# A decoder layer on one core: layer norm a slot ahead, PV of self-attention a slot back, maximum, output copy and PV in another order

## The chip, the cores and the metric

The kernel runs on one core of a Trainium2 chip. The time is device time in microseconds (us) of one execution, median over runs. The core has five engines with queues of their own: TensorE (PE, matmuls; PEld is its weight load), VectorE (DVE), ScalarE (ACT), GpSimd (POOL) and SyncE (SP, which starts the DMAs). Each queue is worked off strictly in its order, and an instruction that waits for a semaphore holds up all that stand behind it on its engine.

## The reference

A pre-norm decoder layer on 2048 tokens of width 256 (16 sequences of 128), in float32:

```
x = x + self_attention(layernorm(x))     # 4 batches of 512 tokens, 16 heads of 64
x = x + cross_attention(layernorm(x), ctx)   # 16 heads of 16, keys and values from ctx, mask
x = x + moe_ffn(layernorm(x))            # sum over 8 experts of width 512 (gelu), times a gate factor
```

Each attention is softmax(Q K^T / sqrt(d)) V, then an output projection with bias. A query attends the 128 tokens of its own sequence, so an attention block is 128 by 128. The kernel takes the tokens as groups 0 to 3 of 512 tokens, each of 4 tiles of 128.

## The kernel before, in words

**Halves.** TensorE works on float32 numbers split in a high and a low half: every matrix product is three matmuls (high-high, high-low, low-high; helper `three`, line 458). So each result in PSUM is copied twice to SBUF: ScalarE writes the high half (`..._hi`, `..._evac`), then VectorE subtracts and writes the low half (`..._low`, `..._lo`). The low half frees the bank.

**Phases and slots.** Phase 0 is self-attention, phase 1 cross-attention, phase 2 the experts. In the first two each of the 4 groups of tokens has 16 slots (PERIOD), and the attention of a group is 16 quads: a quad is a PSUM bank of 4 blocks of 128x128 scores. What each engine does in a slot is written out in four tables, PE_ORDER, ACT_ORDER, DVE_ORDER and POOL_ORDER, each with one row of entries for phase 0 and one for phase 1. An entry has the name of the operation, of the step, and a pair of lags, for phase 0 and phase 1. `steps` (line 229) says which quad or job a step has in slot v: quad q has its scores in slot 7+q in self-attention and in slot 11+q in cross-attention (SCORES), and an operation with lag L comes L slots later. Slots from 16 on are those of the next group, so two groups overlap. `run` goes through the slots: in each it takes the entries in the order of the table, for the earlier groups first. The table of the earlier phase holds in the first 8 slots (TURN) of a phase. After cross-attention's last group follow 20 slots of drain.

**A quad's way.** TensorE: scores into bank S0 or S1 (`scores`). VectorE: row maximum (`row_max`, L910). ScalarE: exponential and row sum (`exp_probs`, L738), which frees the bank. VectorE: reciprocal (`row_inverse`, L915). GpSimd: product with it (`normalise`, L1127). TensorE: transpose into bank T (L537). ScalarE and VectorE: the two halves of PT (L746, L821), double-buffered. TensorE: PV into the one bank O. ScalarE (`out_hi`, L757, L765) and VectorE (`out_low`, L931, L938): the halves of AT. TensorE: output projection (`project_out`) into the banks Y. At the group's end VectorE adds the residual (`add_residual`, L949) and GpSimd the bias (`out_bias`, L1137), after which x_ready is given.

**Jobs beside it.** In self-attention 16 value jobs and 16 query/key jobs of the group run in slots 4 to 19, one of each in a slot; value jobs use the one bank A1, query/key jobs the one bank A0. Even query/key jobs are keys, odd ones queries; their copies (`qk_evac`, L700/L705; `qk_low`, L873/L878) come in the slot after their matmuls, so keys are copied in odd slots. A matmul of job j waits for the low half of job j-1. The value copies are `v_evac` (L720) and `v_low` (L821). V has room for two sets of 4 jobs, and the first copy of a set waits for the PV that reads the old contents last:

```python
if t == 0 and (cp > 1 or not (isinstance(g, int) and g == 0)):
    act.wait_ge(pv_ps, nth(SLOT_F2, ph, g, 4 * (cp - 1) - 1))
```

In cross-attention there are 4 query/key jobs (slots 5, 6, 10, 11) and 2 value jobs. Keys and queries are stacked through DRAM: SyncE writes them out after the low half and reads them back (`stack_keys`, `stack_queries`), and the scores of quads 0 and 8 wait for that (L517).

**Layer norm.** It works ahead for the group: statistics (L825), aggregation (L833, and rstd on GpSimd, L1122), normalisation (`ln_apply`, xn, L847), then the transposes of tokens (`transpose_group`, L599) in slots 3 and 4 with copies XT (L680, L854). GpSimd splits the context of cross-attention in slots 0 to 3 (`split_context`, L1154 and L1160).

Of the kernel before, what the change touches and what calls it, by code (L numbers as in the profile page):

```python
# [80 lines left out]
def build(nc, x, ctxT, mask, pieces, gateT, biases, rows, out):  # L81
    with ExitStack() as ctx:
        def sb(name, shape, dt):
            return ctx.enter_context(nc.sbuf_tensor(name, shape, dt))
# [41 lines left out]
        probs = sb("probs", [P, 4, 512], F32)  # L126
# [6 lines left out]
        bias = sb("bias", [P, NBIAS], F32)  # L133
# [95 lines left out]
        def steps(name, ph, v, lag=0):  # L229


            v -= lag
            if name == "quad":
                q = v - SCORES[ph]
                return [(q,)] if 0 <= q < QUADS else []
            if name == "qk":
                jobs = {XT_AT + 1 + j: j for j in range(16)} if ph == 0 else QK1_SLOTS
                return [(jobs[v],)] if v in jobs else []
            if name == "v":
                j = v - XT_AT - 1  # L240
                if ph == 0:
                    return [(j, 2)] if 0 <= j < 16 else []
                return [V1_SLOTS[v]] if v in V1_SLOTS else []
            if name in ("qk_out", "v_out", "qk_last", "v_last"):

                own = name.endswith("last")
                done = [j[0] for j in steps(name.split("_")[0], ph, v if own else v - 1)
                        if j[-1] or name[0] == "q"]
                return [(j,) for j in done if own == (ph == 0 and j == 15)]
            if name == "proj":  # L250
                q = v - SCORES[ph]
                if ph == 0:
                    return [(q // 2, (2 * (q % 2), 2 * (q % 2) + 1))] if 0 <= q < QUADS else []
                return {8: [(0, (0, 1))], 9: [(0, (2, 3))], 16: [(1, (0, 1))],
                        17: [(1, (2, 3))]}.get(q, [])
            if name == "residual":
                return [()] if v - SCORES[ph] == (QUADS - 1 if ph == 0 else QUADS + 1) else []
            if name == "bias":
                v -= SCORES[ph] + (QUADS if ph == 0 else QUADS + 1)
                return [(v,)] if 0 <= v < 2 else []  # L260
            if name == "stats":
                return [()] if v == 0 else []
            if name == "aggr":
                return [()] if v == 1 else []
            if name == "norm":
                return [()] if v == 2 else []
            if name in ("xt0", "xt1"):
                return [()] if v == XT_AT + int(name[2]) else []
            if name == "ctx":
                return [(v,)] if ph == 1 and 0 <= v < 4 else []  # L270
            raise ValueError(name)

        def run(order, does, ph, g, earlier, slots=PERIOD):

            for n in range(slots):
                for name, what, lags in order[earlier[0][0] if earlier and n < TURN else min(ph, 1)]:
                    for p, gg, v in [(*e, n + (i + 1) * PERIOD) for i, e in reversed([*enumerate(earlier)])] \
                            + [(ph, g, n)]:
                        if p < 2 or name in ("stats", "aggr", "norm", "xt0", "xt1"):
                            for args in steps(what, p, v, lags[min(p, 1)]):  # L280
                                does[name](p, gg, *args)
                if name_extra := does.get("slot"):
                    name_extra(ph, g, n)
# [34 lines left out]
        def weight_slots(n):  # L318
# [10 lines left out]


        PE_ORDER = (
            (("scores", "quad", (0, 0)), ("xt1", "xt1", (0, 0)), ("proj", "proj", (4, 6)),
             ("pv", "quad", (2, 5)), ("transpose", "quad", (1, 3)), ("v", "v", (0, 0)),
             ("qk", "qk", (0, 0)), ("xt0", "xt0", (0, 0))),
            (("scores", "quad", (0, 0)), ("xt1", "xt1", (0, 0)), ("proj", "proj", (4, 6)),
             ("pv", "quad", (2, 5)), ("v", "v", (0, 0)), ("qk", "qk", (0, 0)),
             ("xt0", "xt0", (0, 0)), ("transpose", "quad", (1, 3))))
        ACT_ORDER = (
            (("probs", "quad", (2, 4)), ("xt1", "xt1", (0, 0)), ("v", "v_out", (0, 0)),
             ("qk", "qk_out", (0, 0)), ("exp", "quad", (0, 1)), ("out", "quad", (2, 5)),  # L340
             ("v", "v_last", (0, 0)), ("qk", "qk_last", (0, 0)), ("xt0", "xt0", (0, 0))),
            (("probs", "quad", (2, 4)), ("xt1", "xt1", (0, 0)), ("v", "v_out", (0, 0)),
             ("qk", "qk_out", (0, 0)), ("exp", "quad", (0, 1)), ("out", "quad", (2, 5)),
             ("xt0", "xt0", (0, 0))))
        DVE_ORDER = (
            (("inverse", "quad", (1, 2)), ("out", "quad", (3, 6)), ("probs", "quad", (2, 4)),
             ("xt1", "xt1", (0, 0)), ("max", "quad", (0, 1)), ("residual", "residual", (4, 6)),
             ("v", "v_out", (0, 0)), ("qk", "qk_out", (0, 0)), ("stats", "stats", (0, 0)),
             ("aggr", "aggr", (0, 0)), ("norm", "norm", (0, 0)), ("v", "v_last", (0, 0)),
             ("qk", "qk_last", (0, 0)), ("xt0", "xt0", (0, 0))),  # L350
            (("max", "quad", (0, 1)), ("inverse", "quad", (1, 2)), ("out", "quad", (3, 6)),
             ("probs", "quad", (2, 4)), ("xt1", "xt1", (0, 0)), ("residual", "residual", (4, 6)),
             ("v", "v_out", (0, 0)), ("qk", "qk_out", (0, 0)), ("stats", "stats", (0, 0)),
             ("aggr", "aggr", (0, 0)), ("norm", "norm", (0, 0)), ("xt0", "xt0", (0, 0))))
        POOL_ORDER = (
            (("normalise", "quad", (1, 2)), ("bias", "bias", (4, 6)), ("ctx", "ctx", (0, 0)),
             ("aggr", "aggr", (0, 0))),
            (("normalise", "quad", (1, 2)), ("bias", "bias", (4, 6)), ("aggr", "aggr", (0, 0)),
             ("ctx", "ctx", (0, 0))))

        block = ctx.enter_context(nc.Block())
# [887 lines left out]
```

## Time and profile before

| what | value |
|---|---|
| median of 3 runs | 988.9 us (988.74 to 991.47) |
| the profiled execution | 989.09 us, span 987.3 us |
| TensorE, matmul busy | 892.8 us (90%) |
| VectorE busy | 584.4 us (59%) |
| ScalarE busy | 652.7 us (66%) |
| GpSimd busy | 205.4 us (21%) |
| mean granted TensorE clock | 0.973 |

Self-attention runs to about 320 us, its last quads overlap with the start of cross-attention, whose scores start at 374 us and which ends at about 605 us. The experts take the rest. A time in a row is counted from the span's start. A row of a timeline has the start, the time taken, engine, line of the kernel, operation, output and inputs; where the engine stood idle before it, the idle time and what ended it follow in brackets. Some matmuls are missing from the records, so a gap of TensorE without a releaser need not be one.

### The profile page before, as it was taken

The page shows a single profiled execution, that of the slowest core. Times are in us where ns is not written, and L with a number is a line of the kernel's source. Part 1 is how long each engine was busy: PE and PEld are TensorE (multiplying, and loading weights), DVE is VectorE, ACT ScalarE, POOL GpSimd, SP SyncE. Part 2 cuts the span into 40 slices and gives each one's busy share as a digit, 9 for nine tenths or more (in the row PEclk, how much of TensorE's full clock was granted, in tenths as well). Part 3 has the DMA queues.
Part 4 walks back from the last instruction along what each step waited for, and adds up shares of the span by engine and source line. Part 5 has one row for each costly group of instructions (what it writes and reads, how often), then busy time and mean ns, then how long its engine had stood idle before and what let it go on. Part 6 is the DMA issues. An engine that isn't in the chain of part 4 may idle for free.

```text
span 987.3 us, 19148 instructions
## 1 busy us (share of the span) xinstructions
PE 892.8 (90%) x6624; PEld 806.1 (82%) x6624; DVE 584.4 (59%) x1190; ACT 652.7 (66%) x1843; POOL 205.4 (21%) x194
## 2 busy tenths in 40 slices
PE   3899999999999977777888878999999999999997
PEld 2788889889899866676777767999999999999996
DVE  5788788788787854657685776545423332333222
ACT  3797888888888755766677786676455445444543
POOL 3112232132223533425243352000000000000000
PEclk9999999999999997998998989999999999999999
DMA  7210000000000035171543701331000000000000
GB/s 237 94 47 1 2 2 1 0 0 1 0 0 0 2 85 150 34 180 24 149 86 74 181 2 53 98 96 54 22 0 1 0 21 0 0 0 22 2 1 22
DMA packets 21904, 43.07 MB, mean 44 GB/s; under 512 B 3152, under 2 KB 3152, under 8 KB 21712
## 3 DMA queue, kind: packets, MB, share of 16 engines
q1 hardware_dynamic: 21264, 41.95, 15.4%
q8 instruction: 31, 0.51, 0.2%
q10 hardware_dynamic: 576, 0.33, 0.2%
q14 instruction: 33, 0.27, 0.1%
HBM read 31.79 MB, written 10.49 MB: 43 GB/s over the span
## 4 chain that ended last, share of the span: by engine, by line
PE 65%; DVE 13%; ACT 9%; DMA 5%; issue 4%; SPq 2%; DVEq 0%; ACTq 0%; POOL 0%; POOLq 0%
PE A L458 22%; PE Y L458 21%; PE S L458 12%; PE O L458 5%; ACT probs L738 4%; DMA stage<-arena 3%; PE T L537 3%; DVE nm L910 2%; DVE PT L821 2%; DMA arena<-stage 2%; DVE arena L878 2%; DVE xn L847 1%; DVE arena L931 1%; ACT arena L757 1%; SPq L410 1%
## 5 line engine op out<-in xcount | busy, mean ns | idle before, releaser
L821 DVE TENSOR_TENSOR PT<-probs,PT 128x512 fp32r<-128x512 f32 x128 | 89.7, 701 | 230.6 <-ACT PT L801 230.6
L458 PE MATMUL A<-XT,arena 128*128 128x512 f32 x816 | 219.1, 404 | 7.8 <-DVE arena L878 4.9
L738 ACT ACTIVATE probs<-S,nm 128x128 f32<-128x128 f32 x512 | 181.1, 369 | 50.9 <-DVE nm L910 49.6
L1127 POOL TENSOR_TENSOR probs<-probs,rinv 128x512 f32<-128x512 f32 x128 | 133.4, 1042 | 372.2 <-DVE rinv L915 372.2
L458 PEld LDWEIGHTS Y<-arena,PT 128*128 128x128 f32 x1536 | 200.3, 191 | 11.0 <-DVE PT L821 1.1
L458 PE MATMUL Y<-arena,PT 128*128 128x256 f32 x1536 | 204.1, 283 | 0.3
L458 PEld LDWEIGHTS A<-XT,arena 128*128 128x128 f32 x816 | 146.3, 192 | 38.6 <-DVE arena L878 7.5
L458 PE MATMUL O<-PT,arena 128*64 128x128 f32 (+1 forms) x1536 | 119.4, 229 | 25.6 <-DVE arena L938 12.3
L801 ACT ACTIVATE PT<-probs 128x512 fp32r<-128x512 f32 x128 | 80.8, 631 | 90.6 <-PE Y L458 90.2
L458 PEld LDWEIGHTS O<-PT,arena 128*64 128x64 f32 (+1 forms) x1536 | 109.1, 126 | 33.2 <-issue 13.5
L821 DVE TENSOR_TENSOR PT<-T,PT 128x512 fp32r<-128x512 f32 x128 | 88.1, 688 | 48.1 <-ACT PT L746 45.9
L746 ACT ACTIVATE PT<-T 128x512 fp32r<-128x512 f32 x128 | 76.5, 598 | 46.0 <-PE T L537 41.9
L738 ACT ACTIVATION_READ_ACCUMULATOR probs<-S,nm 128x1 f32 x512 | 106.3, 208 | 0.0
L910 DVE TENSOR_REDUCE nm<-S 128x4 f32<-128x512 f32 x128 | 87.5, 684 | 18.7 <-PE S L529 11.8
L458 PE MATMUL S<-XT,arena 128*128 128x512 f32 x384 | 98.4, 393 | 0.0
L537 PE MATMUL T<-ident,probs 128*128 128x128 f32 x512 | 82.4, 285 | 7.7 <-DVE PT L821 7.2
L458 PEld LDWEIGHTS S<-XT,arena 128*128 128x128 f32 x384 | 68.3, 189 | 11.4
L931 DVE SCALAR_TENSOR_TENSOR arena<-O,bias,arena 64x256 fp32r<-64x256 f32 x128 | 60.8, 475 | 26.4 <-ACT arena L757 25.0
L458 PE MATMUL Y<-arena 128*128 128x256 f32 x480 | 70.7, 284 | 1.5 <-DVE arena L938 1.5
L797 ACT ACTIVATE probs<-A,bias 128x512 f32<-128x512 f32 x64 | 44.0, 687 | 41.6 <-PE A L458 41.6
L458 PE MATMUL A<-arena,XT 128*128 128x256 f32 x384 | 62.9, 301 | 8.4 <-DVE XT L854 5.3
L797 ACT ACTIVATE probs<-S,bias 128x512 f32<-128x512 f32 x64 | 44.0, 688 | 39.3 <-PE S L458 39.2
(92 smaller groups left out, 1119.9 us busy)
## 6 DMA issues: line engine op xcount, KB each, us to landing
wst<-in_pieces SPq DMA_DIRECT2D x52, 256.0 KB, 2.6
stage<-arena SPq DMA_DIRECT2D x32, 256.0 KB, 3.4
arena<-stage SPq DMA_DIRECT2D x48, 128.0 KB, 4.1
arena<-stage SPq DMA_DIRECT2D x24, 256.0 KB, 3.8
xs<-in_x SPq DMA_DIRECT2D x4, 512.0 KB, 5.0
craw<-in_ctxT SPq DMA_DIRECT2D x4, 512.0 KB, 4.9
out<-craw SPq DMA_DIRECT2D x4, 512.0 KB, 2.6
probs<-in_rows SPq DMA_DIRECT2D x1, 1024.0 KB, 8.1
```

What stands on the lines that cost most here:

```text
L410: sp.dma_start(KS[32 * i + 16 * h:32 * i + 16 * h + 16, r, :, h, :].bitcast(F32), stage[r, 0, s].rearrange("(u h d) t -> h d u t", h=2, d= ...
L458: mm = pe.matmul(acc, lhs[a], rhs[b], start=first and i == 0, stop=last and i == 2, skip_group_check=shared)
L537: mm = pe.transpose(T[:, u * P:(u + 1) * P], probs[:, n % 4, u * P:(u + 1) * P], ident[:, :])
L738: last = act.activation(probs[:, n % 4, u * P:(u + 1) * P], S[n % 2][:, u * P:(u + 1) * P], ACT.Exp, bias=nm[:, n % 4, u:u + 1], accum_out ...
L746: act.activation(PT[:, n % 2, 0, :], T[:, :], ACT.Copy).then_inc(pt_hi, 1)
L797: act.activation(probs[:, m % 4, :], H[m % 4][:, :], ACT.Gelu, bias=bias[:, B1 + m:B1 + m + 1]).then_inc(act_done, 1)
L801: act.activation(PT[:, m % 2, 0, :], probs[:, m % 4, :], ACT.Copy).then_inc(h_hi, 1)
L821: dve.tensor_tensor(out_, src, hi.bitcast(F32), ALU.subtract).then_inc(sem_, 1)
L878: last = dve.scalar_tensor_tensor(K[rows_, c % 2, 1, :, h, :], A0[rows_, :].rearrange("p (b c) -> p b c", b=TILES), bias[rows_, BK1 + c:BK ...
L910: dve.tensor_reduce(nm[:, n % 4, :], s3, axis=AX.X, op=ALU.max, negate=True).then_inc(maxed, 1)
L931: last = dve.scalar_tensor_tensor(AT[rows_, c % 2, 1, cols].rearrange("p (b c) -> p b c", b=2), o4[0:DH1, :, h, :], bias[0:DH1, BV1 + 2 * ...
L1127: pool.tensor_tensor(p3, p3, rinv[:, n % 4, :].unsqueeze(2).to_broadcast([P, 4, P]), ALU.mult).then_inc(normed, 1)
```

## The change

Only the tables and the slots of the layer norm change.

- The aggregation moves from slot 1 to slot 0, behind the statistics; the normalisation from slot 2 to slot 1. This holds for all phases that run through the slots.
- Self-attention: PV has lag 3 instead of 2, and with it the high half of O lag 3 instead of 2, its low half 4 instead of 3, projection, residual and bias 5 instead of 4. On TensorE PV now stands ahead of the projection.
- Cross-attention: the maximum has lag 0 instead of 1 and stands behind the low half of PT (`probs`) instead of at the head of the slot. On VectorE the low half of O now stands ahead of the reciprocal.

```diff
--- before.py
+++ after.py
@@ -261,9 +261,9 @@
             if name == "stats":
                 return [()] if v == 0 else []
             if name == "aggr":
+                return [()] if v == 0 else []
+            if name == "norm":
                 return [()] if v == 1 else []
-            if name == "norm":
-                return [()] if v == 2 else []
             if name in ("xt0", "xt1"):
                 return [()] if v == XT_AT + int(name[2]) else []
             if name == "ctx":
@@ -329,33 +329,33 @@
 
 
         PE_ORDER = (
-            (("scores", "quad", (0, 0)), ("xt1", "xt1", (0, 0)), ("proj", "proj", (4, 6)),
-             ("pv", "quad", (2, 5)), ("transpose", "quad", (1, 3)), ("v", "v", (0, 0)),
+            (("scores", "quad", (0, 0)), ("xt1", "xt1", (0, 0)), ("pv", "quad", (3, 5)),
+             ("proj", "proj", (5, 6)), ("transpose", "quad", (1, 3)), ("v", "v", (0, 0)),
              ("qk", "qk", (0, 0)), ("xt0", "xt0", (0, 0))),
-            (("scores", "quad", (0, 0)), ("xt1", "xt1", (0, 0)), ("proj", "proj", (4, 6)),
-             ("pv", "quad", (2, 5)), ("v", "v", (0, 0)), ("qk", "qk", (0, 0)),
+            (("scores", "quad", (0, 0)), ("xt1", "xt1", (0, 0)), ("proj", "proj", (5, 6)),
+             ("pv", "quad", (3, 5)), ("v", "v", (0, 0)), ("qk", "qk", (0, 0)),
              ("xt0", "xt0", (0, 0)), ("transpose", "quad", (1, 3))))
         ACT_ORDER = (
             (("probs", "quad", (2, 4)), ("xt1", "xt1", (0, 0)), ("v", "v_out", (0, 0)),
-             ("qk", "qk_out", (0, 0)), ("exp", "quad", (0, 1)), ("out", "quad", (2, 5)),
+             ("qk", "qk_out", (0, 0)), ("exp", "quad", (0, 1)), ("out", "quad", (3, 5)),
              ("v", "v_last", (0, 0)), ("qk", "qk_last", (0, 0)), ("xt0", "xt0", (0, 0))),
             (("probs", "quad", (2, 4)), ("xt1", "xt1", (0, 0)), ("v", "v_out", (0, 0)),
-             ("qk", "qk_out", (0, 0)), ("exp", "quad", (0, 1)), ("out", "quad", (2, 5)),
+             ("qk", "qk_out", (0, 0)), ("exp", "quad", (0, 1)), ("out", "quad", (3, 5)),
              ("xt0", "xt0", (0, 0))))
         DVE_ORDER = (
-            (("inverse", "quad", (1, 2)), ("out", "quad", (3, 6)), ("probs", "quad", (2, 4)),
-             ("xt1", "xt1", (0, 0)), ("max", "quad", (0, 1)), ("residual", "residual", (4, 6)),
+            (("inverse", "quad", (1, 2)), ("out", "quad", (4, 6)), ("probs", "quad", (2, 4)),
+             ("xt1", "xt1", (0, 0)), ("max", "quad", (0, 0)), ("residual", "residual", (5, 6)),
              ("v", "v_out", (0, 0)), ("qk", "qk_out", (0, 0)), ("stats", "stats", (0, 0)),
              ("aggr", "aggr", (0, 0)), ("norm", "norm", (0, 0)), ("v", "v_last", (0, 0)),
              ("qk", "qk_last", (0, 0)), ("xt0", "xt0", (0, 0))),
-            (("max", "quad", (0, 1)), ("inverse", "quad", (1, 2)), ("out", "quad", (3, 6)),
-             ("probs", "quad", (2, 4)), ("xt1", "xt1", (0, 0)), ("residual", "residual", (4, 6)),
+            (("out", "quad", (4, 6)), ("inverse", "quad", (1, 2)), ("probs", "quad", (2, 4)),
+             ("max", "quad", (0, 0)), ("xt1", "xt1", (0, 0)), ("residual", "residual", (5, 6)),
              ("v", "v_out", (0, 0)), ("qk", "qk_out", (0, 0)), ("stats", "stats", (0, 0)),
              ("aggr", "aggr", (0, 0)), ("norm", "norm", (0, 0)), ("xt0", "xt0", (0, 0))))
         POOL_ORDER = (
-            (("normalise", "quad", (1, 2)), ("bias", "bias", (4, 6)), ("ctx", "ctx", (0, 0)),
+            (("normalise", "quad", (1, 2)), ("bias", "bias", (5, 6)), ("ctx", "ctx", (0, 0)),
              ("aggr", "aggr", (0, 0))),
-            (("normalise", "quad", (1, 2)), ("bias", "bias", (4, 6)), ("aggr", "aggr", (0, 0)),
+            (("normalise", "quad", (1, 2)), ("bias", "bias", (5, 6)), ("aggr", "aggr", (0, 0)),
              ("ctx", "ctx", (0, 0))))
 
         block = ctx.enter_context(nc.Block())
```

## Rows read from the trace of the kernel before

**Rows 1.** Windows by stage: stretch, its length, busy us per engine, granted clock, DMA.

```profile
17.00:320.00 303.00, 287.05 (x2286) 261.14 (x2286) 242.68 (x495) 250.61 (x792) 69.44 (x66) 0.99 0.05 17
374.00:605.00 231.00, 187.10 (x1569) 165.37 (x1570) 151.98 (x309) 162.59 (x635) 90.35 (x86) 0.90 0.37 90
```

**Rows 2.** Timeline of one key slot of self-attention: start, us, engine, line, operation.

```profile
203.98 0.38 ACT L720 ACTIVATE arena<-A 128x256 fp32r<-128x256 f32 x1
204.19 0.88 PE L458 MATMUL S<-arena 128*128 128x256 f32 x6
204.39 1.38 ACT L705 ACTIVATE arena<-A,bias 64x512 fp32r<-64x512 f32 x2
...
204.90 0.88 PE L458 MATMUL Y<-arena 128*128 128x256 f32 x6
...
205.62 0.88 PE L458 MATMUL O<-PT,arena 128*64 128x128 f32 x12
...
206.04 1.50 DVE L878 SCALAR_TENSOR_TENSOR arena<-A,bias,arena 64x512 fp32r<-64x512 f32 x2
...
207.21 0.95 ACT L757 ACTIVATE arena<-O,bias 64x256 fp32r<-64x256 f32 x2
...
207.60 1.65 PE L458 MATMUL A<-XT,arena 128*128 128x512 f32 x6
...
209.09 0.40 PE L458 MATMUL S<-arena 128*128 128x256 f32 x2
```

**Rows 3.** Timeline of the slot after it, with the residual.

```profile
210.85 1.29 DVE L949 TENSOR_TENSOR xs<-Y,xs 128x512 f32 x2 [0.15 <-PE Y L458]
...
213.35 1.55 PE L458 MATMUL A<-XT,arena 128*128 128x512 f32 x6
```

**Rows 4.** Timeline of self-attention's layer norm, VectorE, in two groups of tokens.

```profile
160.07 1.39 DVE L825 BATCH_NORM_STATS2 st<-xs 128x6 f32 x4
...
165.64 0.38 DVE L833 BATCH_NORM_AGGREGATE mv<-st 128x2 f32<-128x6 f32 x4
...
251.49 1.37 DVE L847 TENSOR_SCALAR xn<-xs,mv,rstd 128x256 f32 x4
```

**Rows 5.** Timeline of slot 11 of cross-attention's group 0.

```profile
369.66 0.75 DVE L884 SCALAR_TENSOR_TENSOR arena<-A,bias,arena 128x512 fp32r<-128x512 f32 x1 [0.83 <-ACT arena L709]
...
374.22 0.77 PE L517 MATMUL S<-dropped,identr 128*128 128x512 f32 x1 [5.32 <-DMA arena<-stage]
...
375.21 2.76 PE L458 MATMUL A<-XT,arena 128*128 128x512 f32 x6
```

**Rows 6.** Timeline of slots 2 to 4 of cross-attention's group 3.

```profile
512.60 1.27 DVE L949 TENSOR_TENSOR xs<-Y,xs 128x512 f32 x2
...
513.80 3.27 DVE L847 TENSOR_SCALAR xn<-xs,mv,rstd 128x256 f32 x4
...
514.17 1.47 POOL L1137 TENSOR_TENSOR xs<-xs,rowc 128x512 f32 x1 [1.04 <-DVE xs L949]
515.60 1.31 POOL L1160 TENSOR_TENSOR CT<-craw,CT 128x512 fp32r<-128x512 f32 x1
...
517.69 0.37 ACT L738 ACTIVATE probs<-S,nm 128x128 f32<-128x128 f32 x1 [3.59 <-DVE nm L910]
...
520.56 0.69 DVE L854 TENSOR_TENSOR XT<-A,XT 128x512 fp32r<-128x512 f32 x1 [2.24 <-ACT XT L680]
...
521.96 0.74 DVE L938 SCALAR_TENSOR_TENSOR arena<-O,bias,arena 32x512 fp32r<-32x512 f32 x1
```

**Rows 7.** Windows: slots 0 to 5 (group 1, group 3, drain), and a low-clock stretch.

```profile
388.40:409.90 21.50, 15.39 (x130) 13.03 (x128) 16.28 (x37) 15.42 (x60) 11.48 (x12) 0.92 0.04 11
505.00:528.90 23.90, 18.79 (x144) 16.26 (x142) 18.85 (x40) 15.42 (x60) 13.93 (x14) 0.79 0.10 26
562.20:582.50 20.30, 16.05 (x137) 13.96 (x135) 16.09 (x39) 14.96 (x60) 9.96 (x9) 0.83 0.26 76
461.00:469.00 8.00, 6.03 (x38) 5.24 (x39) 4.85 (x10) 5.94 (x22) 4.87 (x5) 0.58 0.01 2
```

## The prediction

> **What bounds the kernel now.** The windows by stage come first [rows 1]. TensorE is busy 287 of 303 us in self-attention. In cross-attention it is busy 187 of 231 us at a mean granted clock of 0.90. So self-attention has no room for a new wait of TensorE, and cross-attention has 44 us of idle time and some low clock in which something can be won. The feed-forward part that follows is not touched by the change.
>
> One slot of self-attention shows why TensorE waits for nobody there, and how narrowly [rows 2]. The scores start at 204.19, the output projection 0.71 later, PV at 205.62, the query projection of this slot at 207.60, and the next slot starts at 209.09: 4.90 us. That projection overwrites bank A0, so it needs the low half of the key job before, which VectorE ends at 206.04+1.50=207.54. The margin is 0.06 us. Whatever makes the key job's two copies later makes TensorE later by the same amount. Only odd slots have a key job there; the query job of an even slot has one copy of half the length.
>
> **Part 1: self-attention's PV a slot later.** PV of quad n moves from slot n+9 to n+10. Its gates move with it: the copy of the O bank (ACT, now lag 3, DVE, now lag 4), the projection (lag 5), residual and bias. Between these the distances stay as they are. One user stays put: ScalarE's copy of value job 4c (v_evac, when t is 0), in slot 4c+5, overwrites half of V, and waits for PV of quad 4c-5. That PV was in slot 4c+4. It is now in slot 4c+5, the same one. The wait has been there all along, but PV ended at 205.62+0.88=206.50 and the copy of the next slot comes at 203.98+4.90=208.88, 2.4 us behind. That cover is now gone.
>
> When does it end? In the slot of [rows 2] PV will stand second: start 204.90, end 0.88 later, 205.78, and a waiting engine starts about 0.05 later, 205.83. ScalarE was ready at 203.98. So it stands 1.85 us, with the key copy queued behind it. Key copy: 205.83 plus at most the 0.41 at which it follows the value copy, so about 206.2, and 1.38 long: 207.55. VectorE then needs 1.50: 209.05 instead of 207.54, and the query projection starts at 209.1 instead of 207.60: 1.5 us later. The value job itself doesn't matter: its low half comes a key copy earlier than that.
>
> Is this given back? TensorE's next scores start 1.5 us later too, at about 210.5. ScalarE does its exponentials (1.4, the time from the key copy's end at 205.77 to the O copy at 207.21) from 207.6 to 209.0, the O copy (0.95) to 209.95, VectorE the low half of O, about 1.0, to 210.95, and PV of the next slot stands at 211.2: no further wait. But neither does anything run shorter in the next slot, since TensorE is full. So each occurrence costs its whole amount. How many: c=2, 3 in group 0, and four in each of groups 1 to 3 (the last falls into slot 1 of cross-attention's first group): 2+12=14. Three of them stand in slot 5, behind the slots with the token transposes, where the slot runs late already, so I take 1.4 for the mean: 14 x 1.4 = 19.6. Bounds for one: 0.9, if VectorE's own lateness hides part, and 1.85, the whole wait of ScalarE.
>
> The residual moves from slot 10 to 11, from a query slot to a key slot. Now it starts 1.76 after the scores and the query projection 4.26 after them (213.35-209.09) [rows 2, 3], against 3.41 in the slot of [rows 2], so it costs 0.85. After the change the projection ends 0.72 later in its slot, so the residual starts at 2.5, ends at 3.7, then the value half 0.35 and the key half 1.50: 5.55, and TensorE goes on at 5.6 instead of 3.41. That is 2.2 against 0.85: 1.35 x 3 groups = 4.0 (bounds 0 and 6.5).
>
> **Part 2: layer norm a slot earlier in self-attention.** Slot 0 gets the aggregation (0.38 and one small operation) behind the statistics (1.39), slot 1 the normalisation (1.37) in place of it [rows 4]. So VectorE, busy 243 of 303 us as it is [rows 1], has 3.3 us of layer norm in two slots instead of three, and slot 1 is a key slot. The low half of O comes 0.6 later in slot 1, after the moment at which PV, now second, wants it (0.5 of wait), and the maximum of slot 2 comes late by some 0.9, most of it hidden behind the wait of part 1. I take 0.8 for each of three groups: 2.4 (bounds 0 and 4.5, which is 1.5 each). The transposes of tokens are in slots 3 and 4 as before and don't wait for the norm in self-attention, so nothing is won there.
>
> **Part 3: the passage to cross-attention.** Slot 11 of its first group starts with a wait for the stacked keys and queries, a chain of DMAs [rows 5]: TensorE stands 5.32 us and starts at 374.22; the key job's low half was long done (369.66), so the query projection starts 0.99 later. Three things now come into this slot ahead of that low half on VectorE: the maximum of this slot's scores (was at the head of slot 12), and the residual, which waits for the last projection, itself now behind the waiting scores. Scores 1.2, projection up to 2.65 at the clock of 0.5 that [rows 5]'s matmuls show, residual 1.29, low half 0.75: 4.7 instead of 0.99. Price 3.7 (bounds 0.9, the maximum alone, and 4.5). In groups 1 to 3 only the maximum comes between: 0.9 x 3 = 2.7 (bounds 0 and 4). In slot 6 of groups 1 to 3 the maximum stands ahead of the first key job's low half, and the DMA chain that ends in slot 11 starts with that one: 0.65 x 3 = 2.0 (bounds 0 and 2.1).
>
> **Part 4: what cross-attention wins.** In groups 2 and 3 the residual of the group before and the normalisation share slot 2 [rows 6]: 1.27 and 3.27 us on VectorE in one piece, the maximum behind them, and ScalarE stands 3.59 us for it. Then the token copy is waited for 2.24 us, and TensorE falls to a granted clock of 0.58 for 8 us [rows 7]. After the change the normalisation is in slot 1, the residual alone in slot 2, and each slot's maximum stands ahead of both. I walk VectorE from 506.6, where its PT half of slot 0 ends (maximum, PT half and value half at 0.6 each, as they follow each other, O's low half 0.75, reciprocal 0.1): slot 0 (maximum, value half, statistics, aggregation) 3.3, slot 1 (reciprocal, PT half, maximum, normalisation 2.4) 3.8, slot 2 with the residual 3.3, slot 3 1.3: at 518.3 it is ready for the token copy. ScalarE, whose exponentials no longer stand 3.59 us, delivers at about 519.0, so that it starts then instead of at 520.56, and O's low half follows at 519.7 instead of 521.96, as the maximum isn't between them. That is 2.2 us, and full clock instead of half in slots 4 and 5 gives a good 1 us more: 3.5 each. Group 1 has no residual there: 1.7. The drain has the four normalisations at 1.37 already: 1.2. Together 3.5+3.5+1.7+1.2 = 9.9. Upper bound: VectorE's busy time in the six-slot stretches leaves 5.2, 5.1 (twice) and 4.2 us [rows 7], 19.6 in all; lower bound 2.
>
> The normalisation took 3.27 us where GpSimd's 1.47 and 1.31 us ran beside it, and 1.37 where none did [rows 4, 6]; beside GpSimd's product (1.04) and its copy (0.61) in slot 1 no row shows it, so I take 2.4, between the two. The Trainium skill (SBUF — State Buffer, Who interferes with whom) speaks against more: VectorE's two-port modes and GpSimd take a shared port pair exclusively, for a whole instruction each. By that rule a product and a copy would block it too, which makes 1.37+1.65=3.0, and the gain 0.6 smaller in each of three groups, 1.8 in the sum.
>
> Elsewhere the maximum's earlier place gives nothing: ScalarE waits for it in the slots of the layer norm, and in the others its exponentials come a slot later anyway. O's low half ahead of the reciprocal delays GpSimd's product by about 1.4 us, which has a whole slot of cover.
>
> **The sum.** 19.6 + 4.0 + 2.4 + 3.7 + 2.7 + 2.0 - 9.9 = +24.5. The profiled execution took 989.1 (span 987.3): 1013.6. The median of the runs is 988.9, 0.2 below, so I say 1013.
>
> **Rivals.** (B) Faster: cross-attention's gain is the whole 19.6, and the wait in part 1 is hidden. Then -19.6 + 4.0+2.4+3.7+2.7+2.0 = -4.8: 984. It decides as soon as an occurrence costs TensorE less than 4.8/14=0.34 us. For it: the clock of 0.58 behind the 3.59 us wait is a real loss. Against it: the margin of 0.06 us in [rows 2]. Chance 0.11. (C) Half: each occurrence costs 0.8 and the residual nothing, since engines run ahead of each other more than a single slot shows: 24.5-8.4-4.0=12.1: 1001. Chance 0.12. (D) The waits of 1.5 us lower TensorE's clock in self-attention as the longer one did in cross-attention: 8 us at 0.58 hold 4.6 us of full-speed work, 3.4 lost each, 14 x 3.4=48 more: 1061. Against it: the mean clock of self-attention is 0.99 though it has 16 us of idle time in pieces [rows 1], and no single wait of 1.5 us takes more than a third of a slot. Chance 0.04. The Trainium skill (TensorE: Matmul & The Clock Gate, HAM oscillation) says that waits between groups of matmuls can take the clock down again and again. (E) Self-attention loses about what cross-attention wins, with the wait partly hidden: within 0.3% (about 3 us, what a measurement of this kernel can tell): 989, chance 0.05. The forecast itself: 0.68, its own range 1003 to 1023.
>
> Chances: slower 0.68+0.12+0.04=0.84, same 0.05, faster 0.11. The range leaves out B, D and E and reaches down into C for part-hidden waits: 995 to 1025.
>
> **What would show it.** In the profile after, the waits should hold a new line, ScalarE's V copy (L720) for PV, some 14 times 1.8 us, and TensorE's A for the key half (L878) some 20 us. Part 2 and the residual: slot 11 lasts about 7 us in self-attention. Part 4: no wait of ScalarE over 3 us for the maximum in cross-attention, and a granted clock near 1 in slots 4 and 5. I am wrong if the stage to 320 us is not some 20 us longer, or if cross-attention's stretch shrinks by over 10.

## The result

The changed kernel takes 1015.7 us (median of 4 runs, 1012.0 to 1018.0) against 988.8 for the one before: ratio 1.0284, 95% interval 1.0248 to 1.0320 (the ratio is the one on record; the quotient of the two medians is 1.0271). The forecast was 1013, slower, with a range of 995 to 1025. The profiled execution of the changed kernel took 1018.0 us (span 1016.0).

The windows of the changed kernel, by stage (length, busy time of each engine, granted clock), the answer to [rows 1]. Self-attention's end is set where the first slot of cross-attention's group 0 starts, 320.7 before and 348.3 here:

```profile
17.00:347.60 330.60, 292.25 (x2267) 263.68 (x2268) 244.60 (x493) 250.16 (x790) 69.36 (x66) 0.98 0.05 15
404.00:634.00 230.00, 183.33 (x1579) 161.34 (x1580) 151.73 (x312) 161.66 (x635) 91.29 (x88) 0.93 0.38 90
```

TensorE is busy 5.2 us more, in a stage 27.6 us longer, and VectorE and ScalarE within 2 us of before: waits were added, hardly any work. Cross-attention, from 404 us, is 230 us long against 231, at a clock of 0.93 against 0.90.

Three lines of the waits up to 400 us of the changed kernel (who waited for whom, total, times, longest). The first is not among the waits before; the others were 7.5 (13 times) and 4.9 (13 times) there:

```profile
ACT arena L720 <- PE O L458: 25.1, 14, 2.1
...
PEld A L458 <- DVE arena L878: 29.9, 26, 2.6
...
PE A L458 <- DVE arena L878: 24.5, 25, 2.4
```

Fourteen times ScalarE's value copy stands for PV, 1.8 us each, and TensorE stands 19.6 us more than before for the key's low half (24.5 less 4.9). One such slot in the timeline, the answer to [rows 2]:

```profile
218.16 0.87 PE L458 MATMUL S<-arena 128*128 128x256 f32 x6
...
218.88 0.88 PE L458 MATMUL O<-PT,arena 128*64 128x128 f32 x12
...
219.85 0.38 ACT L720 ACTIVATE arena<-A 128x256 fp32r<-128x256 f32 x1 [1.83 <-PE O L458]
220.13 1.36 ACT L705 ACTIVATE arena<-A,bias 64x512 fp32r<-64x512 f32 x2
...
221.53 1.51 DVE L878 SCALAR_TENSOR_TENSOR arena<-A,bias,arena 64x512 fp32r<-64x512 f32 x2 [0.84 <-ACT arena L705]
...
223.10 1.66 PE L458 MATMUL A<-XT,arena 128*128 128x512 f32 x6 [1.38 <-DVE arena L878]
```

PV is second and ends at 219.76; 0.09 later the value copy starts, 1.83 us after ScalarE was free, and key copy, low half and query projection follow one another without a gap. The projection starts 4.94 after the scores, against 3.41 in [rows 2]; the next slot starts at 224.59, 6.43 after this one instead of 4.90: 1.53.

The slot of self-attention with the residual, the answer to [rows 3]:

```profile
229.32 0.87 PE L458 MATMUL S<-arena 128*128 128x256 f32 x6
...
231.84 1.29 DVE L949 TENSOR_TENSOR xs<-Y,xs 128x512 f32 x2 [0.92 <-PE Y L458]
...
233.38 1.50 DVE L878 SCALAR_TENSOR_TENSOR arena<-A,bias,arena 64x512 fp32r<-64x512 f32 x2
...
234.94 1.65 PE L458 MATMUL A<-XT,arena 128*128 128x512 f32 x6 [0.45 <-DVE arena L878]
```

5.62 from scores to projection (forecast 5.6). The passage, slot 11 of cross-attention's group 0, the answer to [rows 5]:

```profile
404.20 0.77 PE L517 MATMUL S<-dropped,identr 128*128 128x512 f32 x1 [5.50 <-DMA arena<-stage]
...
406.71 1.29 DVE L949 TENSOR_TENSOR xs<-Y,xs 128x512 f32<-128x512 f32 x2 [0.59 <-PE Y L458]
407.92 0.74 DVE L884 SCALAR_TENSOR_TENSOR arena<-A,bias,arena 128x512 fp32r<-128x512 f32 x1
...
408.71 2.93 PE L458 MATMUL A<-XT,arena 128*128 128x512 f32 x6 [2.04 <-DVE arena L884]
```

4.51 instead of 0.99. And slots 1 to 4 of group 3, the answer to [rows 6], where the normalisation now stands alone in slot 1 and the residual alone in slot 2:

```profile
543.64 2.55 DVE L847 TENSOR_SCALAR xn<-xs,mv,rstd 128x256 f32 x4
...
544.02 1.08 POOL L1127 TENSOR_TENSOR probs<-probs,rinv 128x512 f32<-128x512 f32 x1
...
546.90 0.91 PE L458 MATMUL O<-PT,arena 128*32 128x128 f32 x12 [1.82 <-DVE arena L938]
...
548.03 1.27 DVE L949 TENSOR_TENSOR xs<-Y,xs 128x512 f32 x2
...
551.67 0.69 DVE L854 TENSOR_TENSOR XT<-A,XT 128x512 fp32r<-128x512 f32 x1 [1.11 <-ACT XT L680]
...
552.37 0.74 DVE L938 SCALAR_TENSOR_TENSOR arena<-O,bias,arena 32x512 fp32r<-32x512 f32 x1
```

ScalarE's wait of 3.59 us is gone: of its waits for the maximum in cross-attention, 15.3 us before, 0.7 us is left. The windows of slots 0 to 5 (group 1, group 3, drain), the answer to [rows 7]:

```profile
421.80:442.70 20.90, 14.39 (x130) 12.73 (x129) 15.58 (x35) 15.14 (x60) 10.77 (x11) 0.92 0.11 24
537.50:557.40 19.90, 14.85 (x141) 12.90 (x140) 17.30 (x39) 15.34 (x60) 13.13 (x13) 1.00 0.12 25
592.50:611.20 18.70, 13.74 (x137) 11.97 (x135) 16.80 (x39) 14.69 (x60) 9.71 (x9) 1.00 0.30 84
```

### The profile page after: what moved, and what is told of

Same layout as the page of the kernel before. It is cut to its first block, busy times and chain, and to the rows that moved or that the text cites. A ratio compares the mean times of both kernels' runs of the same rounds, so it can differ in the third digit from the quotient of the medians.

```text
span 1016.0 us, 19157 instructions
## 1 busy us (share of the span) xinstructions
PE 896.3 (88%) x6624; PEld 806.6 (79%) x6624; DVE 583.9 (57%) x1190; ACT 652.2 (64%) x1843; POOL 203.9 (20%) x194
## 3 DMA queue, kind: packets, MB, share of 16 engines
q1 hardware_dynamic: 21264, 41.95, 15.3%
## 4 chain that ended last, share of the span: by engine, by line
PE 64%; DVE 15%; ACT 9%; DMA 5%; issue 5%; SPq 2%; DVEq 0%; ACTq 0%; POOL 0%; POOLq 0%
PE A L458 21%; PE Y L458 20%; PE S L458 12%; PE O L458 5%; PE T L537 3%; DMA stage<-arena 3%; DVE arena L878 3%; ACT probs L738 3%; ACT arena L705 2%; DVE PT L821 2%; DMA arena<-stage 2%; DVE nm L910 2%; DVE arena L931 2%; DVE xn L847 1%; SPq L410 1%
## 5 line engine op out<-in xcount | busy, mean ns | idle before, releaser
L458 PE MATMUL A<-XT,arena 128*128 128x512 f32 x816 | 224.4, 412 | 33.1 <-DVE arena L878 24.5
L458 PEld LDWEIGHTS A<-XT,arena 128*128 128x128 f32 x816 | 149.1, 195 | 66.1 <-DVE arena L878 29.9
L458 PE MATMUL O<-PT,arena 128*64 128x128 f32 (+1 forms) x1536 | 115.6, 225 | 30.7 <-DVE arena L938 18.4
L458 PEld LDWEIGHTS O<-PT,arena 128*64 128x64 f32 (+1 forms) x1536 | 105.0, 123 | 39.3 <-issue 29.0
L738 ACT ACTIVATION_READ_ACCUMULATOR probs<-S,nm 128x1 f32 x512 | 108.4, 212 | 0.0
L458 PE MATMUL Y<-arena 128*128 128x256 f32 x480 | 74.7, 292 | 1.5 <-DVE arena L938 1.5
L537 PEld LDWEIGHTS T<-ident,probs 128*128 128x128 f32 x512 | 59.8, 145 | 15.5 <-issue 9.9
```

Source lines behind the costliest of these rows:

```text
L458: mm = pe.matmul(acc, lhs[a], rhs[b], start=first and i == 0, stop=last and i == 2, skip_group_check=shared)
L537: mm = pe.transpose(T[:, u * P:(u + 1) * P], probs[:, n % 4, u * P:(u + 1) * P], ident[:, :])
L738: last = act.activation(probs[:, n % 4, u * P:(u + 1) * P], S[n % 2][:, u * P:(u + 1) * P], ACT.Exp, bias=nm[:, n % 4, u:u + 1], accum_out ...
```

## The experiments

Theory A is the forecast's: the value copy's wait for PV, passed on by the key copy. A slot's length is the distance from its scores to those of the next slot. Below, "cross" is the time from the first L517 matmul to the start of the last exponential of cross-attention, "start" where it begins, both read from the timelines. Before: start 374.2, cross 222.9. Changed: 404.2 and 221.8. Both come from a single execution each. Each run's ratio is against the kernel before on the same chip.

**e1: the wait taken away, all else as changed.** Tile t of V is read by even quads for t below 2 and by odd ones above, so each pair of tiles needs its own PV:

```diff
-if t == 0 and (cp > 1 or not (isinstance(g, int) and g == 0)):
-    act.wait_ge(pv_ps, nth(SLOT_F2, ph, g, 4 * (cp - 1) - 1))
+if t % 2 == 0 and (cp > 1 or not (isinstance(g, int) and g == 0)):
+    act.wait_ge(pv_ps, nth(SLOT_F2, ph, g, 4 * (cp - 1) - (1 if t else 2)))
```

> The changed kernel, and in ScalarE's value copy one thing else: the first job of a set of V (t=0) waits for PV of quad 4c-6, the last that reads tiles 0 and 1, and the third (t=2) for PV of quad 4c-5, which reads tiles 2 and 3 last. Both are done a slot before the copy, so the wait of ScalarE is gone while PV, its lags and all orders stay as changed. Theory A (the wait of the value copy for PV, passed on through the key copy, is most of the loss): 14 x 1.5 = 20 us less than the changed kernel, 995 to 997 against 1015.7. Theory B (the loss is in the moved work itself: PV ahead of the projection, O's low half late, the residual in a key slot): within 5 us of the changed kernel, 1010 to 1016.

Measured: 996.0 us, ratio 1.0088 (1.0054 to 1.0122); start 383.3, 20.9 earlier than in the changed kernel. The waits show no value copy waiting for PV, and of TensorE for the key's low half this is left:

```profile
PE A L458 <- DVE arena L878: 6.3, 17, 1.9
```

The same kind of slot:

```profile
208.53 0.87 PE L458 MATMUL S<-arena 128*128 128x256 f32 x6
208.73 1.38 ACT L705 ACTIVATE arena<-A,bias 64x512 fp32r<-64x512 f32 x2
...
211.94 1.66 PE L458 MATMUL A<-XT,arena 128*128 128x512 f32 x6
...
213.43 0.87 PE L458 MATMUL S<-arena 128*128 128x256 f32 x6
```

4.90 again. Theory A holds: 19.6 of the 26.8 us between the medians hang on this wait. By the slots of the two traces, the 14 slots with the wait are 19.1 us shorter here.

**e6: the wait alone, nothing moved.** In the kernel before:

```diff
-    act.wait_ge(pv_ps, nth(SLOT_F2, ph, g, 4 * (cp - 1) - 1))
+    act.wait_ge(pv_ps, nth(SLOT_F2, ph, g, 4 * (cp - 1)))
```

> The kernel before, where the first value copy of a set waits for PV of quad 4c-4 instead of 4c-5. Nothing is moved: this puts the wait alone into it, on a PV that stands third in its slot (0.72 later than in the changed kernel) in the same 14 slots. Theory A: 14 x (1.5+0.7) = 31 us longer, about 1019. Theory B (ScalarE's wait is absorbed unless PV's lag changes): under 1000.

Measured: 1024.7 us (2 runs), ratio 1.0390 (1.0353 to 1.0428). The start is 409.4, 35.1 later than before, so all of the loss lies in front of cross-attention. Cross is 219.7 against 222.9 although nothing in cross-attention was edited: slots 10 and 11 of its group 1 take 8.7 us together instead of 12.2 (8.4 in e2). So a difference of 3 or 4 us in "cross" between two traces shows nothing by itself.

```profile
ACT arena L720 <- PE O L458: 32.5, 14, 2.5
```

Slots 9 and 13 take 7.15 us where they took 4.90, slots 1 and 5 are 1.9 to 2.0 longer: about 29 us for the 14, a little under the 31 expected. What is left to 35 stands mostly at slots of 8.3 to 8.4 us, where TensorE was granted half its clock for a few us (mean 0.76 from 202 to 209 us); the expectation did not have that.

**e2: PV's move alone.** The kernel before with lags 3, 4 and 5 and PV ahead of the projection:

```diff
-(("scores", "quad", (0, 0)), ("xt1", "xt1", (0, 0)), ("proj", "proj", (4, 6)),
- ("pv", "quad", (2, 5)), ...
+(("scores", "quad", (0, 0)), ("xt1", "xt1", (0, 0)), ("pv", "quad", (3, 5)),
+ ("proj", "proj", (5, 6)), ...
```

> The kernel before with only self-attention's PV, its copies, projection, residual and bias a slot later, and PV ahead of the projection. Theory A: 19.6 for the value copy's wait, 4.0 for the residual in the key slot; the passage costs 2.8 at most without the maximum ahead of the key's low half: 1013 to 1016. Theory B as to the place, but with layer norm and maximum needed for it (the three parts slow each other down): under 1005.

Measured: 1011.9 us, ratio 1.0224 (1.0189 to 1.0259), 1 us under the range of theory A. The other two parts of the change aren't needed for the loss: the 14 slots are 19.2 us longer. Slot 11 at the passage lasts 7.24 us here too, without the maximum in it: that price is the residual's.

**e3 and e4: layer norm alone, maximum alone.** e3 is the kernel before with aggregation in slot 0 and normalisation in slot 1; e4 has the maximum's new lag in both rows of DVE_ORDER and the new order of cross-attention's row, with O's low half at its old lag (but, as in the change, ahead of the reciprocal).

> The kernel before with only the layer norm a slot earlier. Theory A (the collision of residual and normalisation in slot 2 is what cross-attention loses): cross-attention 5 to 8 us shorter, self-attention 1 to 2.5 us longer, 982 to 986. Theory C (it is the maximum's place at the head of the next slot, behind whatever VectorE has in hand, that costs, and the layer norm alone only moves the stall a slot ahead): 987 to 991.

> The kernel before with only cross-attention's maximum in its own slot behind PT's low half, and O's low half ahead of the reciprocal. Theory A: the keys' low half comes later behind the maximum in slots 6 and 11 (+2.0 and +3.6), and the maximum no longer stands behind the normalisation (a gain of 3 to 5, as ScalarE's 3.6 us of wait in groups 2 and 3 goes, but the normalisation still stands in front of O's low half and the token copy): 986 to 991. Theory C: most of the gain of cross-attention is here, 979 to 984.

Measured: e3 988.6, ratio 1.0011 (0.9990 to 1.0032); e4 987.5, ratio 0.9977 (0.9956 to 0.9999). The medians alone would fit theory C for e3 and theory A for e4. The slots say more. Cross-attention's slots by place, in us, summed over the groups (slots 0 to 5 of groups 1 to 3 and of the drain; slot 6 and slot 10 of groups 1 to 3; slot 11 of groups 0 to 3):

| kernel | slots 0 to 5 | slot 6 | slot 10 | slot 11 |
|---|---|---|---|---|
| before | 89.3 | 12.5 | 17.9 | 14.4 |
| e6 (cross-attention as before) | 89.2 | 12.5 | 16.0 | 13.1 |
| e2 (as before, residual in the passage) | 89.6 | 12.5 | 15.4 | 16.7 |
| e3 (layer norm) | 88.9 | 12.5 | 15.8 | 12.5 |
| e4 (maximum) | 79.3 | 14.3 | 18.3 | 22.0 |
| e5 (both) | 79.9 | 14.3 | 18.2 | 20.2 |
| changed | 79.8 | 14.3 | 16.5 | 22.5 |
| e7 (both, keys first) | 79.8 | 12.5 | 16.7 | 12.7 |

Where the code is the same (before, e6, e2), slots 0 to 5 agree within 0.4 us, while slots 10 and 11 differ. The layer norm alone wins 0.4 in slots 0 to 5: nothing that can be told. e4's order wins 10.0, all that the whole change wins there, with residual and normalisation still together in slot 2. ScalarE's waits for the maximum from the first scores of cross-attention to 605 us (total, times, longest), before, in e3 and in e4:

```profile
ACT probs L738 <- DVE nm L910: 15.3, 12, 3.6
...
ACT probs L738 <- DVE nm L910: 13.5, 15, 1.6
...
ACT probs L738 <- DVE nm L910: 0.2, 1, 0.2
```

So the layer norm alone splits the stall and moves it a slot ahead, as theory C has it, and the maximum's place takes it away. e4's total is hardly better than before because the same order costs slots 6 and 11 what it wins (1.8 and 7.6). Whether it is the maximum or O's low half ahead of the reciprocal that wins in slots 0 to 5, no run separates.

In self-attention e3's slots 0 to 3 of group 2 take 5.07, 5.74, 5.06 and 5.62 instead of 5.03, 5.13, 4.71 and 5.31, 1.3 for each of three groups; it starts cross-attention at 379.5, 5.3 later, of which 1.5 arose before group 1's first slot, where other runs differ by up to 0.8 without a cause in their tables. Cross is 219.0, 3.9 less than before, but 3.7 of that are slots 10 and 11 of group 1, which differ as much without any edit (e6).

**e5: both, PV put back.** The changed kernel with self-attention's lags 2, 3 and 4 and the projection ahead of PV.

> The changed kernel with self-attention's PV, its copies, projection, residual and bias put back where they were: what is left is the layer norm a slot earlier and cross-attention's new order. The layer norm alone gained 4 us in cross-attention and lost 5 ahead of it, the maximum alone gained about 2 in cross-attention. Theory A (they act on one stall: with the normalisation a slot earlier and the maximum ahead of it, nothing of VectorE's is left in front of ScalarE's exponentials; together as in the changed kernel, six slots of groups 2 and 3 in 20 us instead of 23.7): more than the sum of the two, 9 us gained there, 4.7 given back in slots 6 and 11, 5 lost ahead: 988 to 990 against 988.6, cross-attention from its first to its last scores 3 to 5 us shorter. Rival (the gains add, or one of them has the whole gain): cross-attention 6 to 7 us shorter, or 2.

Measured: 988.0, ratio 1.0018 (0.9999 to 1.0038); start 379.4, cross 218.8, 4.1 less than before. The total is that of theory A, but not its reason: slots 0 to 5 win 9.4, no more than e4 alone (10.0). That is the rival's second case, one of the two has the whole gain: it is e4's order, and the earlier layer norm adds nothing to it that can be told.

**e7: keys ahead of the maximum.** As e5, in cross-attention's row of DVE_ORDER:

```diff
- ("max", "quad", (0, 0)), ("xt1", "xt1", (0, 0)), ("residual", "residual", (4, 6)),
- ("v", "v_out", (0, 0)), ("qk", "qk_out", (0, 0)), ...
+ ("qk", "qk_out", (0, 0)), ("max", "quad", (0, 0)), ("xt1", "xt1", (0, 0)),
+ ("residual", "residual", (4, 6)), ("v", "v_out", (0, 0)), ...
```

> As e5, and on VectorE in cross-attention the low half of keys and queries stands ahead of the maximum. Theory A (the maximum in front of the keys' low half costs 0.65 in slot 6, where the DMA chain to slot 11 starts, and 0.9 to 1.8 in slot 11, where the scores it needs wait for those DMAs): 0.65 x 3 + 0.9 x 3 + 1.8 = 6.5 at most off e5, 982 to 985. Rival (slots 6 and 11 are hidden behind the DMA chain): as e5.

Measured: 981.7, ratio 0.9956 (0.9939 to 0.9973). Slot 6 of groups 1 to 3 takes 4.14 to 4.20 instead of 4.76, slot 11 3.06 instead of 4.0 to 5.5. By the medians it is 6.3 under e5, and 6.5 was the most expected. In the traces cross is 209.1, 9.7 less than e5, all of it in slots 6, 10 and 11 (1.8, 1.5 and 7.5, less 1 elsewhere); slots 6 and 11 are back at what they take in the kernels without the change's order (e3, e6), and slots 0 to 5 are those of e5. So the maximum's earlier place pays once it doesn't stand in front of the keys; in the change the one ate the other.

**e9: the residual behind the jobs' copies.** As e1, and in both rows of DVE_ORDER the residual comes after "v" and "qk":

```diff
- ("residual", "residual", (5, 6)), ("v", "v_out", (0, 0)), ("qk", "qk_out", (0, 0)), ...
+ ("v", "v_out", (0, 0)), ("qk", "qk_out", (0, 0)), ("residual", "residual", (5, 6)), ...
```

> As e1 (the changed kernel with the value copy waiting by tile), and on VectorE the residual stands behind the copies of the value and key jobs in both attentions. Theory A (the residual now falls into a key slot, slot 11 lasts 7.11 instead of 4.90 us three times, and it stands in front of the key's low half at the passage, 7.24 instead of 3.55): 3 x 2.2 and about 2 at the passage, 8 to 9 us off e1's 996.0: 986 to 989. Rival (slot 11 is long because the projection and PV are there, not through the residual's place): 993 to 996.

Measured: 984.2, ratio 0.9969 (0.9945 to 0.9992), 11.8 under e1. Theory A, with more than it asked for: the start is 7.3 earlier and the passage's slot 11 2.7 shorter (4.54 instead of 7.24); where the rest comes from is not shown. Slot 11 of self-attention's group 2, with the residual, which VectorE now does after the key half, and the start of the next slot:

```profile
215.12 0.87 PE L458 MATMUL S<-arena 128*128 128x256 f32 x6
...
216.97 1.51 DVE L878 SCALAR_TENSOR_TENSOR arena<-A,bias,arena 64x512 fp32r<-64x512 f32 x2
...
218.51 1.29 DVE L949 TENSOR_TENSOR xs<-Y,xs 128x512 f32 x2
...
220.03 0.87 PE L458 MATMUL S<-arena 128*128 128x256 f32 x6
```

4.91 instead of 7.11.

**e8 and e10: a version faster than both.** e8 is e7 with self-attention's layer norm back in slots 1 and 2 and its residual behind the jobs' copies:

```diff
 if name == "aggr":
-    return [()] if v == 0 else []
+    return [()] if v == (1 if ph == 0 else 0) else []
 if name == "norm":
-    return [()] if v == 1 else []
+    return [()] if v == (2 if ph == 0 else 1) else []
```

e10 is e8 with PV a slot later as in the change and e1's wait.

> As e7, with self-attention's layer norm back in slots 1 and 2 (only cross-attention's and the experts' stay a slot earlier) and self-attention's residual behind the copies of the jobs on VectorE. Theory A: the earlier layer norm costs self-attention 1.3 us a group (slots 0 to 3 last 21.5 instead of 20.2) and the residual 0.9 a group: 4 to 6 us off e7, 977 to 981. Rival (the layer norm's place only shifts the late slots): within 1 us of e7.

> As e8, with self-attention's PV and what follows it a slot later as in the change, and the value copy waiting by tile, so that the later PV makes nobody wait. It asks what the later PV is worth by itself. Theory A (self-attention is full with TensorE's own work, so an order in which nobody waits can't give more): within 2 us of e8's 974.3. Rival (PV a slot later takes PT's low half out of TensorE's way in slots 4 and 5, where 6.9 and 5.8 us are spent instead of 4.8): 3 to 6 us below e8.

Measured: e8 974.3, ratio 0.9886 (0.9859 to 0.9912); e10 974.3, ratio 0.9843 (0.9801 to 0.9885). e8's windows, self-attention and cross-attention:

```profile
17.00:323.00 306.00, 291.73 (x2326) 265.99 (x2327) 247.09 (x505) 254.44 (x805) 70.49 (x67) 0.99 0.05 16
372.50:592.00 219.50, 177.97 (x1578) 157.38 (x1578) 149.84 (x309) 162.08 (x636) 88.90 (x86) 0.95 0.40 95
```

Cross-attention's scores start at 372.8 (374.2 before), cross is 210.6 (222.9 before). e8 is 7.4 under e7, more than the 4 to 6 expected: groups 1 to 3 of self-attention are 2.1 to 2.4 us shorter each, and the expectation's own terms, 1.3 and 0.9 a group, make 6.6. Between e8 and e10 no difference can be told: the medians are equal, the two intervals overlap, and groups 2 and 3 of self-attention take 81.0 us (e8) and 80.9 to 81.0 us (e10). A later PV that makes nobody wait is worth nothing here, within what these runs can tell.

## Why the prediction was right

Its step was the right one, and most terms came out at their size. One reason behind a term did not hold, and one rival that it nearly ruled out did occur, in small. Slot lengths of self-attention are those of group 2.

| step | forecast | measured |
|---|---|---|
| value copy's wait, per slot | 1.5; 1.4 in the mean of 14 | changed less e1: 1.53 in slots 9 and 13, 1.20 in slot 5, 1.29 in slot 1; 1.37 in the mean |
| the same, in all | 19.6 | 19.1 by the slots, 19.6 by the medians (changed less e1) |
| residual in slot 11 instead of 10 | 1.35 a group | +2.21 in slot 11, -0.92 in slot 10: 1.29 |
| layer norm in self-attention | 0.8 a group | slots 0 to 3, changed less e2: 0.9 |
| query projection in the passage's slot | 3.7 later | 3.5 later; slot 7.24 instead of 3.55 |
| slot 6, slot 11 in groups 1 to 3 | 0.65, 0.9 | 0.6; 1.0, 2.5 and 0.9 |
| cross-attention's slots 0 to 5 | -1.7, -3.5, -3.5, -1.2 | -0.6, -3.6, -3.8, -1.6 |
| normalisation in slot 1 | 2.4 | 2.55 |

The slots 0 to 5 of cross-attention add up to -9.6 (forecast -9.9). Slot 11 cost 1.7 more than forecast in groups 1 to 3, and slot 10, which had no term, gave 1.3 back. Up to cross-attention's start the terms make 26.0, and the trace has 30.0; from there on they make -1.5, and the trace has -1.1. The forecast was 2.7 us short of the median; the profiled execution itself is 2.4 above its median.

The missing 4 us are, as far as the trace goes, rival D's mechanism, three times instead of fourteen. The clock in self-attention is 0.98 against 0.99 in the mean, but it fell twice, both times in slot 11 with the residual, after TensorE had stood 1.4 us for the value half and 0.45 us for the key half, and once more in slot 5 of cross-attention's first group. The granted clock in the two stretches, and the query projection in the first:

```profile
143.00:148.00 5.00, 4.55 (x24) 3.78 (x22) 2.86 (x7) 1.07 (x2) 2.29 (x2) 0.66 0.02 3
324.00:329.00 5.00, 4.56 (x26) 3.95 (x26) 2.81 (x6) 1.07 (x2) 2.28 (x2) 0.66 0.00 0
...
143.95 2.93 PE L458 MATMUL A<-XT,arena 128*128 128x512 f32 x6 [0.45 <-DVE arena L878]
```

It takes 1.66 at full clock. These slots last 8.34 and 8.15 us instead of group 2's 7.11, which with the slots behind them is 1.5 us each. The same wait in group 2 did not do it, nor did the 14 value slots here; in e6, with longer waits there, the clock fell beside them too. The forecast priced an occurrence at 3.4 us and all 14 at 48, so D's size was wrong both ways. In cross-attention the clock fell behind the 5.5 us wait at the passage, as before.

Part 4 had the right size with a reason that only half held, and that part of the match is luck. It starts from the residual and the normalisation in one slot and counts on both moves: separating them, and each slot's maximum ahead of them. Separating them alone (e3) wins 0.4 us in slots 0 to 5; the new order alone (e4), with both still in slot 2, wins 10.0. In group 1, where there is no such collision, e4 wins 3.4 and the whole change 0.6.

Also not as forecast: alone, the layer norm costs self-attention 1.3 a group (e3), against 0.9 beside the waits of part 1 (changed less e2). The passage was put down to maximum and residual; e2 shows the residual alone makes slot 11 7.24 long, the maximum alone 5.36 (e4), and they don't add. That the maximum's place gives nothing elsewhere held: what e7 wins over e5 lies in slots 6, 10 and 11, where the prediction had put its price, and only slot 11's price was sized too small. No run has the keys first with the old layer norm.

Rival B needed an occurrence to cost less than 0.34 us; it cost 1.4. Of the port rule (the Trainium skill, SBUF — State Buffer, Who interferes with whom) the trace agrees in kind: the four normalisations, 0.4 us each without GpSimd, took 0.57, 1.12, 0.69 and 0.40, and each of the first three ended 0.15 us after the GpSimd instruction that ran beside it. The 3.0 for the four together, a normalisation's whole length on top of GpSimd's each time, was too much: they took 2.55.

## What to carry to other kernels

When an operation moves by a slot, list not only what it waits for but everyone who waits for it at a fixed slot: a wait that never cost anything has a margin, and here it was 2.4 us, half a slot. Its price is then read where the waiting engine's next work is needed, not at the waiting instruction. Waits written for a whole buffer can be cut to the part that is overwritten, which here gave back 20 us without moving anything; and in an order written by hand, what frees a single bank for TensorE goes ahead of what is needed only later (e7, e9). And a median that doesn't move can hide a gain and a loss of 10 us each, as in e4: compare the slots, with an unedited run beside them to see how far a single trace can be trusted.

## What the runs showed of the hardware

Repeated runs of the kernel before lay between 982.0 and 992.2 us, so that differences of 2 us needed the intervals. After the 5.3 us wait for a DMA, TensorE ran at 1.2 GHz well past its next matmuls (granted clock 0.50 from 374 to 386 us): the query projection took 2.76 us [rows 5], 1.65 at full clock [rows 2]. That wait is 4.3 to 6.2 us in all twelve versions, though its start moves between 372 and 409 us: none took it away.

Waits of TensorE of 1.4 and 0.45 us close together, in a slot of 7.1 us, took the clock to 1.2 GHz in some groups and not in others (two of three in the changed kernel, one of three in e1 and in e2); each time cost about 1.5 us. A VectorE instruction beside a GpSimd one took 1.12 us instead of 0.4 and ended 0.15 us after it.
